# Attention outputs normalised by GpSimd instead of VectorE, with a new written-out order of the attention stage

## The chip, the cores and the metric

The kernel runs on one core of a Trainium2 chip. The metric is the device time of one execution in microseconds (us): the median of three runs, for the kernel before and for the changed kernel. The engines are named as in the profile: PE is TensorE (matmuls; PEld its weight loads), DVE is VectorE, ACT is ScalarE, POOL is GpSimd, SP is SyncE, whose queue issues the DMAs here.

## What is computed

A chain of four blocks over 1024 tokens of 512 features, each with a residual and a layer norm: a state-space scan, a gated feed-forward network, causal attention, and a feed-forward network with 4-bit weights. The change is inside the attention block:

```python
n_head = 32                      # head size 16, T = 1024, one sequence
q, k, v = proj(wq), proj(wk), proj(wv)
q, k = rope(q), rope(k)
scores = q @ k.T / 4             # causal: -inf above the diagonal
attn = softmax(scores)
out = (attn @ v) @ wo.T
```

## The kernel before

Before the attention stage the queries and keys lie in SBUF with the features of a head down the partitions (`q_st`, `k_st`): each pair of heads takes 128 partitions, one head in the upper 64 and one in the lower. The values lie by token (`v_tok`). The stage works on eight groups `g` of four heads, and on each group in two halves of 512 queries. Softmax takes the exact row maximum, so for a half the work has these steps; the letter is the one that stands for the step in the order string.

- `s`, search: PE multiplies a tile of 128 queries with up to 512 keys of a head (`search`, L741; on the diagonal two small matmuls add a mask, L745) into one of three PSUM banks (0 to 2, the "ring"), and DVE takes the row maximum from there (`maxima`, L1651). A group needs 12 searches for the first half and 28 for the second, 40 in all; those of group 0 are done earlier, beside the projections. 280 remain for the stage.
- `n`: DVE joins the maxima of the two key halves (`negate`, L1681). `t`: PE turns the maxima into a row in a ring bank (`turn_maxima`, L755), DVE copies it to SBUF (`keep_rows`, L1658), and two DMAs on SP's queue (`put_rows`, L427) put it into rows of `q_st`, so that the next matmul subtracts it.
- `k`, keys: PE multiplies a tile of 128 keys with the queries of the half for two or four heads (`keys`, L794) into banks 3 and 4, or 5 and 6, in turn; ACT takes the exponential (`exponentials`, L1178) into one of four buffers `p_t`. On the diagonal GpSimd zeroes a corner (`cut_corner`, L1322). For the last, narrowest tile of a half (`j` = 3 or 7) the four heads fill just 256 of the 512 columns of each of the two banks.
- `v`, values: PE multiplies the exponentials with the values and a column of ones (`values`, L810), summed over the half's key tiles in bank 7. The values come from `v_ring`, which GpSimd copies for a group (`ring_values`, L1315). Behind the last tile ACT copies bank 7 to `o_raw` (`keep_out`, L1164).
- `o`, out: PE transposes `o_raw` in four 128x128 pieces into a ring bank (`turn_out`, L819); DVE takes the reciprocal of the sums (`divide`, L1686) and multiplies (L1688) into `o_tok`.

Every engine walks the same list `ORDER` and does its own share of each step, so the list is the order of PE's queue and of the others'. It is made from three strings, HEAD, PATTERN (three times) and TAIL. Letters `x`, `y`, `z` near the end are DVE's dequantising of the first weight tiles of the last block (`nibbles`, `unscaled`, `weights_low`); GpSimd's multiplies with the scales (L1333, L1335) belong to them. Semaphores carry the waits: `ring_full` and `ring_read` for the ring, `st_full` and `exp_done` for the keys banks, `pv_step` for the values, `o_kept` for `o_raw`. The stage ends with PE transposing `o_tok` (L859), which waits until all outputs are read.

## Time and profile before

| | us |
|---|---|
| median of 3 runs | 849.19 (848.98 to 850.1) |
| the profiled execution, whole | 853.84 |
| its span, first to last instruction | 852.1 |
| attention stage in it (first keys to last output) | about 442 to 645 |

The profile is one execution. The page gives busy time by engine; views of the trace give the same for a stretch, for groups of like instructions, and instruction by instruction. A row names the source line, engine, operation, tiles written and read, shapes, and a count. In a timeline a row that merges several instructions gives the start of the first and the time until the end of the last. PSUM is `ps`, and most of SBUF is one tile, `arena`.

### The profile page before, as it was taken

Reading aid. Unit: us, or ns where it says so; the run is one execution under the profiler, and the core shown is the slowest. Engines: PE = TensorE matmul, PEld = TensorE weight load, DVE = VectorE, ACT = ScalarE, POOL = GpSimd, SP = SyncE. Lnnn points to the kernel's source line nnn. Section 1 sums busy time; section 2 is a strip of 40 time slices with the busy share of each in tenths; the row PEclk is TensorE's granted clock in tenths of the full one; section 3 lists DMA queues with packets and bytes.
Section 4 is the critical chain, followed back from the end, with each engine's and each line's share of the span. In section 5 each row is a group of like instructions: output and inputs, shape, how many; then the busy total and the mean of one; then the engine's idle time right before and its main releaser. Section 6 shows DMA issues by size and latency. Waiting matters only on the chain.

```text
span 852.1 us, 18986 instructions
## 1 busy us (share of the span) xinstructions
PE 788.1 (92%) x7930; PEld 372.6 (44%) x7930; DVE 628.5 (74%) x896; ACT 431.6 (51%) x579; POOL 297.7 (35%) x217
## 2 busy tenths in 40 slices
PE   8659787897999999999999999999998999999997
PEld 2434444444544444444334454444435544444444
DVE  3997999998556334456648999999976787774344
ACT  4876667564854331143236777787794633332100
POOL 0598898993103000058401222211242222221000
PEclk9597999999999999999999999999998999999999
DMA  7900000005331000039800000000232024320001
GB/s 216 379 2 3 3 3 3 3 3 173 99 90 28 1 0 1 1 55 192 149 1 2 2 2 1 2 2 2 63 120 61 1 92 125 124 81 0 13 37 50
DMA packets 53296, 46.62 MB, mean 55 GB/s; under 512 B 38289, under 2 KB 44241, under 8 KB 53218
## 3 DMA queue, kind: packets, MB, share of 16 engines
q1 hardware_dynamic: 53218, 45.49, 18.8%
q8 instruction: 60, 0.98, 0.5%
q14 instruction: 18, 0.15, 0.1%
HBM read 34.87 MB, written 2.16 MB: 43 GB/s over the span
## 4 chain that ended last, share of the span: by engine, by line
PE 71%; DVE 15%; ACT 5%; issue 5%; POOL 3%; SPq 1%; DMA 1%; DVEq 0%; ACTq 0%; POOLq 0%
PE ps L887 13%; PE ps L639 10%; PE ps L662 10%; PE ps L810 7%; DVE arena L1425 7%; PE ps L923 7%; PE ps L741 6%; PE ps L718 6%; PE ps L794 3%; DVE arena L1651 2%; PE ps L745 2%; PE ps L553 2%; PE ps L507 1%; POOL arena L1272 1%; ACT arena L1178 1%
## 5 line engine op out<-in xcount | busy, mean ns | idle before, releaser
L1651 DVE TENSOR_REDUCE arena<-ps 128x1 f16<-128x512 f32 (+3 forms) x320 | 182.4, 631 | 15.2 <-PE ps L741 7.3
L1178 ACT ACTIVATE arena<-ps 128x1024 f32<-128x1024 f32 (+2 forms) x160 | 142.5, 941 | 43.6 <-PE ps L794 42.8
L1272 POOL TENSOR_TENSOR arena<-arena 128x1024 f32<-128x1024 f32 x62 | 145.7, 2376 | 16.7 <-DVE arena L1425 11.5
L1425 DVE TENSOR_TENSOR_SCAN arena<-arena,ps 128x1024 f32<-128x1024 f32 x64 | 142.4, 2271 | 5.6 <-ACT arena L1019 3.0
L887 PE MATMUL ps<-arena 128*128 128x512 f16 x528 | 114.6, 379 | 0.1
L741 PE MATMUL ps<-arena 64*128 64x512 f16 (+3 forms) x384 | 97.1, 330 | 3.2 <-DVE arena L1658 1.2
L662 PE MATMUL ps<-arena 128*128 128x512 f16 (+1 forms) x464 | 97.6, 372 | 1.0 <-ACT arena L1096 1.0
L1322 POOL TENSOR_SCALAR_AFFINE_SELECT arena<-arena 128x512 f32<-128x512 f32 x64 | 42.7, 674 | 142.9 <-ACT arena L1178 142.8
L553 PE MATMUL ps<-arena 64*128 64x64 f16 x3072 | 60.0, 196 | 33.7 <-DVE arena L1425 30.4
L553 PEld LDWEIGHTS ps<-arena 64*128 64x128 f16 x3072 | 52.2, 98 | 85.0 <-DVE arena L1425 73.3
L639 PE MATMUL ps<-arena 128*128 128x512 f16 x384 | 88.8, 383 | 0.0
L1019 ACT ACTIVATE arena<-arena,negA 128x1024 f32<-128x1024 f32 x64 | 72.4, 1146 | 28.8 <-DVE arena L1425 26.9
L810 PE MATMUL ps<-arena 128*32 128x512 f32 (+3 forms) x768 | 82.1, 501 | 3.0 <-POOL arena L1322 3.0
L887 PEld LDWEIGHTS ps<-arena 128*128 128x128 f16 x528 | 51.6, 98 | 62.0 <-DVE arena L1766 0.6
L507 PE MATMUL ps<-arena,ident_sb 64*64 64x512 f32 x512 | 71.4, 633 | 2.1 <-POOL arena L1272 1.4
L794 PE MATMUL ps<-arena 64*128 64x512 f16 (+3 forms) x384 | 68.8, 326 | 0.9 <-ACT arena L1178 0.6
L662 PEld LDWEIGHTS ps<-arena 128*128 128x128 f16 x464 | 45.3, 98 | 51.7 <-ACT arena L1096 1.2
L741 PEld LDWEIGHTS ps<-arena 64*128 64x128 f16 x384 | 30.3, 93 | 71.5 <-DVE arena L1651 45.5
L923 PE MATMUL ps<-arena 128*128 128x512 f16 (+1 forms) x297 | 57.2, 355 | 0.0
L639 PEld LDWEIGHTS ps<-arena 128*128 128x128 f16 x384 | 36.2, 98 | 42.9 <-issue 3.3
L745 PE MATMUL ps<-mask_b,picks_b 64*128 64x64 bf16 (+1 forms) x512 | 53.0, 202 | 0.0
L1281 POOL COPY arena<-arena 128x512 f32 x24 | 14.8, 616 | 100.7 <-DVE arena L1520 46.0
(175 smaller groups left out, 960.7 us busy)
## 6 DMA issues: line engine op xcount, KB each, us to landing
arena<-in_w_q_dram SPq DMA_DIRECT2D x11, 768.0 KB, 4.1
arena<-c_rows SPq DMA_DIRECT2D x16, 512.0 KB, 10.9
arena<-in_w_s_dram SPq DMA_DIRECT2D x11, 384.0 KB, 4.9
arena<-in_x_fm_dram SPq DMA_DIRECT2D x8, 256.0 KB, 4.6
out_dram<-arena SPq DMA_DIRECT2D x8, 256.0 KB, 2.0
arena<-in_wg_dram SPq DMA_DIRECT2D x1, 1792.0 KB, 10.2
arena<-in_wu_dram SPq DMA_DIRECT2D x1, 1792.0 KB, 7.2
arena<-in_wd_dram SPq DMA_DIRECT2D x1, 1792.0 KB, 11.2
```

What stands on the lines that cost most here:

```text
L553: last = nc.tensor.matmul(ps[:, 2 * (i % 2) + r, q * SUB:(q + 1) * SUB], dtx_tok[c % 2][rows, s, q, :], diag[n][rows, e, q, :], start=(k = ...
L639: last = nc.tensor.matmul(banks(bank, 1), part[:, c, ds(t * P, P)], wsp[:, w, s, c, :], start=(c == 0 and part is src_h and s == 0), stop= ...
L662: last = nc.tensor.matmul(banks(bank, 1)[:, lo:hi], w[:, c, m * P:(m + 1) * P], part[:, c, h * HALF + lo:h * HALF + hi], start=(c == 0 and ...
L741: last = nc.tensor.matmul(dst, q_st[rows, 2 * g + r, i * P:(i + 1) * P], k_st[rows, 2 * g + r, key:key + w], start=True, stop=not diag)
L794: last = nc.tensor.matmul(ps[:, 3 + 2 * (e % 2) + b, at * (hi - lo):(at + 1) * (hi - lo)], k_st[rows, 2 * g + r, j * P:(j + 1) * P], q_st[ ...
L810: last = nc.tensor.matmul(ps[32 * a:32 * a + 32, 7, lo - HALF * half:HALF], v_ring[g % 2][:, j, a, :], p_t[n % 4][:, a, 0:hi - lo], start= ...
L887: last = nc.tensor.matmul(banks(bank + h, 1), gu[u][:, s, w * DC + c, :], part[:, c, h * HALF:(h + 1) * HALF], start=(c == 0 and s == 0 an ...
L923: last = nc.tensor.matmul(banks(u, 1)[:, lo:hi], part[:, m, ds(t * P, P)], wd1[:, s, m, lo:hi], start=(m == 0 and part is h1h and s == 0), ...
L1178: nc.scalar.activation(dst, src, ACT.Exp, scale=float(HD) ** -0.5).then_inc(exp_done, 1)
L1272: nc.gpsimd.tensor_tensor(hC[i % 4][:], hst[i % 3][:], c_all[:, n, :], ALU.mult).then_inc(hc_done, 1)
L1425: nc.vector.tensor_tensor_scan(hst[i % 3][:], dA[i % 3][:], banks(2 * (i % 2), 2), 0.0, ALU.mult, ALU.add).then_inc(scan_done, 1)
L1651: nc.vector.reduce_max(maxima_slot(half, k), ps[:, ring_bank(n), 0:len(heads) * w].rearrange("p (a w) -> p a w", a=len(heads)), AX, negate ...
```

## The change

- The outputs of a half no longer go through the ring, but for the last one of the stage. PE puts their four transposes into the free half of the two keys banks, as part of the keys step of the narrowest tile of a later half (`out_beside`: the outputs of (g, 0) beside keys (g, 1, 7), those of (g-1, 1) beside keys (g, 0, 3)). That step waits for `o_kept`.
- ACT copies the transposed outputs to SBUF (`o_copy`) right behind the exponential of that step; the keys step two further on, which writes the same banks, waits for this copy.
- DVE takes only the reciprocal, from SBUF (`invert`); GpSimd multiplies (`divide`), both at the new letter `d`.
- GpSimd walks `ORDER` as well. Its first ring copy is split in seven tiles and one, so that it no longer waits for all eight value tiles, and the copy for group 1 moves behind the first four corners.
- The searches of a half go in their natural order in place of the two written-out orders.
- `ORDER` is one string for the whole stage. ACT's `keep_out` no longer waits for the output of the group before.

```diff
-        r_den = view(199.75, 4 * GH, f32).rearrange("p (i a) -> p i a", i=4)
+        r_den = [view(199.75 + u / 16, 4 * GH, f32).rearrange("p (i a) -> p i a", i=4) for u in range(2)]
+        o_copy = [view(kb, HALF, f32) for kb in (120, 122)]
...
-        UNIT_ORDER = ((0, 1, 6, 8, 7, 3, 2, 9, 4, 11, 10, 5),
-                      (15, 4, 17, 13, 24, 5, 19, 26, 27, 12, 7, 10, 3, 8, 25, 20, 6, 9, 14, 0, 2, 21, 22, 11, 16, 1, 23, 18))
-        SEARCH = [[max_units(half)[k] for k in UNIT_ORDER[half]] for half in range(2)]
+        SEARCH = [max_units(half) for half in range(2)]
...
-        HEAD = ("kknntkkvkvsskssssssvssvsksskokssksskssksnsksvtskssvsskksvssksvskkssvssks"
...
+        ATTENTION = ("kkntssskskssvsksksssksksvkssvksvktssskssvsskkssvskkssvsskssvskssvsskkssskvnskdsssvskssktvsskskss"
...
+                     "svksskdsvsksvvskksssvksskvsksskvssksvtksskssskkssvskskdssvkvkntvkkvkkdxvvkvkkvkkvkvkkkyzvkkkvvvv"
+                     "do")
+
+        def out_beside(g, half, j):
+            if j != 4 * half + 3 or (g, half) == (0, 0):
+                return None
+            return (g, 0) if half else (g - 1, 1)
+        OUTS = 2 * NG - 1
...
                 if e >= 2:
                     pe.wait_ge(exp_done, e - 1)
+                    if out_beside(*EXP_STEP[e - 2]) is not None:
+                        g0, half0 = out_beside(*EXP_STEP[e - 2])
+                        pe.wait_ge(o_copied, 2 * g0 + half0 + 1)
...
+                if out_beside(g, half, j) is not None:
+                    g0, half0 = out_beside(g, half, j)
+                    pe.wait_ge(o_kept, 2 * g0 + half0 + 1)
+                    for b in range(4):
+                        i = 4 * half0 + b
+                        last = nc.tensor.transpose(ps[:, 3 + 2 * (e % 2) + b // 2, HALF // 2 + (b % 2) * P:HALF // 2 + (b % 2 + 1) * P],
+                                                   o_raw[:, i * P:(i + 1) * P], ident_sb[:])
                 last.then_inc(st_full, 1)
...
             pe.wait_ge(ring_read, EARLY + len(IN_RING))
+            pe.wait_ge(o_divided, OUTS)
...
-                if g:
-                    act.wait_ge(ring_read, RING_AT["out", g - 1, half] + 1)
...
+                if out_beside(g, half, j) is not None:
+                    g0, half0 = out_beside(g, half, j)
+                    if g0:
+                        act.wait_ge(o_divided, 2 * g0 + half0 - 1)
+                    nc.scalar.copy(o_copy[half0].rearrange("p (b q) -> p b q", b=2), ps[:, bank:bank + 2, HALF // 2:HALF]).then_inc(o_copied, 1)
...
-            pool.wait_ge(v_proj, TT)
-            pool.wait_ge(v_kept, TT)
...
+            def divide(g, half):
+                pool.wait_ge(r_made, 2 * g + half + 1)
+                src = o_copy[half].rearrange("p (i a d) -> p i a d", i=4, a=GH)
+                nc.gpsimd.tensor_tensor(o_tok[:, 4 * half:4 * half + 4, g * GH * HD:(g + 1) * GH * HD].rearrange("p i (a d) -> p i a d", a=GH),
+                                        src[:, :, :, 0:HD], r_den[half].unsqueeze(3).broadcast_to([P, 4, GH, HD]), ALU.mult).then_inc(o_divided, 1)
...
-            ring_values(0)
-            ring_values(1)
-            for g in range(NG):
-                for j in range(TT):
-                    cut_corner(g, j // 4, j)
-                    if j == 3 and 1 <= g < NG - 1:
-                        ring_values(g + 1)
...
+            ring_values(0, 0, TT - 1)
+            ring_values(0, TT - 1, TT)
+            for kind, g, half, *at in ORDER:
+                if kind == "divide":
+                    divide(g, half)
+                if kind != "keys" or not on_diagonal(half, at[0]) or at[1][-1] != 1:
+                    continue
+                cut_corner(g, half, at[0])
+                if at[0] == 3 and g < NG - 1:
+                    ring_values(g + 1)
...
+            def invert(g, half):
+                dve.wait_ge(o_copied, 2 * g + half + 1)
+                if g:
+                    dve.wait_ge(o_divided, 2 * g + half - 1)
+                src = o_copy[half].rearrange("p (i a d) -> p i a d", i=4, a=GH)
+                nc.vector.reciprocal(r_den[half].unsqueeze(3), src[:, :, :, HD:HD + 1]).then_inc(r_made, 1)
```

## Rows read from the trace of the kernel before

**Rows 1.** The page: the span, and busy us (share of the span) by engine.

```profile
span 852.1 us, 18986 instructions
PE 788.1 (92%) x7930; PEld 372.6 (44%) x7930; DVE 628.5 (74%) x896; ACT 431.6 (51%) x579; POOL 297.7 (35%) x217
```

**Rows 2.** Busy time by stretch: length, each engine's busy us (instructions), PE clock, DMA.

```profile
442.00:449.86 7.86, 5.93 (x57) 2.22 (x56) 0.41 (x2) 4.88 (x6) 2.51 (x5) 1.00 0.01 2
449.86:621.16 171.30, 169.69 (x1839) 75.78 (x1832) 169.09 (x321) 127.11 (x149) 37.44 (x60) 1.00 0.05 15
519.80:544.70 24.90, 24.76 (x275) 11.08 (x272) 24.57 (x48) 18.76 (x22) 5.63 (x10) 1.00 0.01 2
621.16:645.42 24.26, 20.07 (x185) 7.10 (x181) 15.83 (x24) 19.15 (x24) 13.48 (x10) 0.92 0.22 71
```

**Rows 3.** Groups by line and shape, 442 to 645.5 us: busy us, mean ns | idle before.

```profile
L1178 ACT ACTIVATE arena<-ps 128x1024 f32<-128x1024 f32 x112 | 110.0, 1027 | 32.9 <-PE ps L794 32.6 <-issue 0.2
L1651 DVE TENSOR_REDUCE arena<-ps 128x1 f16<-128x512 f32 x168 | 108.2, 684 | 1.2
L1322 POOL TENSOR_SCALAR_AFFINE_SELECT arena<-arena 128x512 f32<-128x512 f32 x64 | 42.7, 674 | 142.9 <-ACT arena L1178 142.8
L1164 ACT COPY arena<-ps 128x512 f32<-128x512 f32 x16 | 9.5, 593 | 7.1 <-PE ps L810 7.0
L1688 DVE TENSOR_TENSOR arena<-ps,arena 128x256 f32<-128x256 f32 x16 | 6.8, 424 | 0.6
```

**Rows 4.** Who waited for whom, 470 to 594.5 us: total us, times, longest.

```profile
PEld ps L741 <- DVE arena L1651: 30.3, 52, 0.8
PEld ps L741 <- DVE arena L1688: 6.7, 8, 0.8
```

**Rows 5.** DVE's instructions in order of time, 519 to 545 us: start, us.

```profile
522.89 0.17 DVE L1681 TENSOR_TENSOR arena<-arena 128x16 f16<-128x16 f16 x1
522.98 1.22 DVE L1651 TENSOR_REDUCE arena<-ps 128x2 f16<-128x256 f32 x3
...
526.74 0.25 DVE L1686 RECIPROCAL arena<-ps 128x16 f32<-128x16 f32 x1
527.02 0.42 DVE L1688 TENSOR_TENSOR arena<-ps,arena 128x256 f32<-128x256 f32 x1
527.48 5.63 DVE L1651 TENSOR_REDUCE arena<-ps 128x1 f16<-128x512 f32 x10
```

**Rows 6.** All engines in order of time at the stage's start, 441 to 462 us.

```profile
444.55 0.60 ACT L1150 ACTIVATE arena<-ps 128x512 f32<-128x512 f32 x1 [0.81 <-PE ps L639]
...
445.28 1.17 POOL L1315 COPY arena<-arena 128x512 f32<-128x512 f32 x2 [26.90 <-ACT arena L1150]
...
445.63 0.41 DVE L1658 COPY arena<-ps 4x512 f16<-4x512 f16 x1 [4.34 <-PE ps L755]
...
449.86 6.80 DVE L1651 TENSOR_REDUCE arena<-ps 128x2 f16<-128x256 f32 x13 [3.82 <-PE ps L745]
```

**Rows 7.** All engines in order of time in the tail, 616 to 646 us.

```profile
622.02 0.41 DVE L1658 COPY arena<-ps 4x512 f16<-4x512 f16 x1 [0.68 <-PE ps L755]
...
622.76 0.86 PE L810 MATMUL ps<-arena 128*32 128x256 f32 x16
...
625.68 0.61 PE L794 MATMUL ps<-arena 64*128 64x512 f16 x4
...
638.07 3.69 POOL L1322 TENSOR_SCALAR_AFFINE_SELECT arena<-arena 128x512 f32<-128x512 f32 x3 [0.84 <-ACT arena L1178]
...
638.60 2.07 DVE L1703 SCALAR_TENSOR_TENSOR arena<-arena 128x1536 f32<-128x1536 int32 x1
```

**Rows 8.** The chain that ended last, 440 to 530 us: values of 256 and 128 columns.

```profile
471.98 0.57 PE ps L810 x8
...
473.64 0.36 PE ps L810 x8
```

**Rows 9.** GpSimd's groups over the whole span, by shape.

```profile
L1302 POOL TENSOR_TENSOR arena<-arena 128x512 f16<-128x512 f32 x16 | 18.6, 1159 | 0.3
```

More of the change, by code:

```diff
@@ L185, in build @@
         st_full, exp_done, p_masked, pv_step, o_kept = sem("st_full"), sem("exp_done"), sem("p_masked"), sem("pv_step"), sem("o_kept")
+        o_copied, o_divided = sem("o_copied"), sem("o_divided")
         o_turned, oh_done, ol_done = sem("o_turned"), sem("oh_done"), sem("ol_done")
@@ L243, in exp_units @@
             return [(0, 1)] if 2 * (hi - lo) <= HALF else [(0,), (1,)]
+        EXP_STEP = [step for step in STEPS for _ in exp_units(*step[1:])]
         EXP_TO = list(itertools.accumulate(len(exp_units(half, j)) for _, half, j in STEPS))
@@ L265, in attention_order @@
                            if g or (half, k) not in EARLY_UNITS]),
-                "n": iter([("negate", g, half) for g, half in halves]),
+                "n": iter([("negate", g, 1) for g in groups]),
                 "t": iter([("turn", g, half) for g, half in halves if g or half]),
-                "o": iter([("out", g, half) for g, half in halves]),
+                "d": iter([("divide", n // 2, n % 2) for n in range(OUTS)]),
+                "o": iter([("out", NG - 1, 1)]),
                 "x": iter([("weights", 0, 0)]), "y": iter([("weights", 1, 0)]), "z": iter([("weights", 2, 0)])}
             order = []
-            for letter in HEAD + 3 * PATTERN + TAIL:
+            for letter in ATTENTION:
                 step = next(streams[letter])
@@ L1306, in _, with ring_values @@
                     stack(2 * k + u, u)
-            pool.wait_ge(v_proj, TT)
-            pool.wait_ge(v_kept, TT)
             pool.wait_ge(v_ones, 2)
-            def ring_values(g):
+            def ring_values(g, lo=0, hi=TT):
                 if g >= 2:
                     pool.wait_ge(pv_step, STEP_AT[g - 1, 0, 0])
-                nc.gpsimd.tensor_copy(v_ring[g % 2][:, :, :, 0:HD],
-                                      v_tok[:, :, g * GH * HD:(g + 1) * GH * HD].rearrange("p i (a d) -> p i a d", a=GH)).then_inc(v_ringed, 1)
+                pool.wait_ge(v_kept, hi)
+                last = nc.gpsimd.tensor_copy(v_ring[g % 2][:, lo:hi, :, 0:HD],
+                                             v_tok[:, lo:hi, g * GH * HD:(g + 1) * GH * HD].rearrange("p i (a d) -> p i a d", a=GH))
+                if hi == TT:
+                    last.then_inc(v_ringed, 1)
+            def divide(g, half):
[3 more added lines that the diff above has]
+                                        src[:, :, :, 0:HD], r_den[half].unsqueeze(3).broadcast_to([P, 4, GH, HD]), ALU.mult).then_inc(o_divided, 1)
             def cut_corner(g, half, j):
@@ L1678, in negate @@
             def negate(g, half):
-                if half:
-                    dve.wait_ge(ring_read, searched(g, 1))
-                    nc.vector.tensor_tensor(m_neg[1][:], m_neg[1][:], m_b[:], ALU.min).then_inc(m_joined, 1)
+                dve.wait_ge(ring_read, searched(g, half))
+                nc.vector.tensor_tensor(m_neg[half][:], m_neg[half][:], m_b[:], ALU.min).then_inc(m_joined, 1)
+            def invert(g, half):
[4 more added lines that the diff above has]
+                nc.vector.reciprocal(r_den[half].unsqueeze(3), src[:, :, :, HD:HD + 1]).then_inc(r_made, 1)
             def divide(g, half, n):
@@ L1685, in divide @@
                 src = ps[:, ring_bank(n), :].rearrange("p (i a d) -> p i a d", i=4, a=GH)
-                nc.vector.reciprocal(r_den[:].unsqueeze(3), src[:, :, :, HD:HD + 1]).then_inc(r_made, 1)
+                nc.vector.reciprocal(r_den[half].unsqueeze(3), src[:, :, :, HD:HD + 1]).then_inc(r_made, 1)
                 dve.wait_ge(r_made, 2 * g + half + 1)
                 nc.vector.tensor_tensor(o_tok[:, 4 * half:4 * half + 4, g * GH * HD:(g + 1) * GH * HD].rearrange("p i (a d) -> p i a d", a=GH),
-                                        src[:, :, :, 0:HD], r_den[:].unsqueeze(3).broadcast_to([P, 4, GH, HD]),
+                                        src[:, :, :, 0:HD], r_den[half].unsqueeze(3).broadcast_to([P, 4, GH, HD]),
                                         ALU.mult).then_inc(ring_read, 1)
@@ L1725, in _ @@
                     keep_rows(g, half, RING_AT[kind, g, half])
+                elif kind == "divide":
+                    invert(g, half)
                 elif kind == "out":
+                    dve.wait_ge(o_divided, OUTS - 1)
                     divide(g, half, RING_AT[kind, g, half])
```

17 lines of the change are left out of this document (7 added, 10 removed).

## The prediction

> **What bounds the kernel now.** I read the page's summary first: PE is busy 92% of 852.1 us, DVE 74% [rows 1]. Such shares are averages over stages, so I next cut the attention stage, the only one that the diff touches, into stretches [rows 2]. The reader is to see there one engine that is full in the long middle stretch: from 449.86 to 621.16 us DVE is busy 169.09 of 171.30 us, and in a settled period of 24.90 us (one group of four heads) 24.57 us. PE shows nearly the same (24.76), but its ends are modelled, so that number can't decide between the two. The waits do [rows 4]: in five periods PE's weight loads for the maxima search (L741) sat 30.3 us behind DVE's reductions (L1651), and 6.7 us more behind the normalising multiply (L1688). PE waits for DVE to empty a ring bank; DVE hardly waits for PE. So this stretch is set by DVE: 280 reductions (40 of them for each of seven groups), the turn copies and the normalising of outputs.
>
> The two ends of the stage have other bounds. At the start DVE stands still until 449.86 us, after its one small copy at 445.63 [rows 6]: PE, in order, has values to do that wait for GpSimd's ring copies, and those began only when ScalarE had kept the eighth value tile. At the end, from 621.16 to 645.42 us, no search is left; ScalarE is busy 19.15 of 24.26 us [rows 2], and the last 7 us are a chain through GpSimd's corners, the last values, copy, transposes and division.
>
> **The change, part by part.**
>
> *Outputs leave the ring.* Today an output costs DVE a reciprocal (starts 526.74), a multiply (527.02) and the next reduction starts at 527.48: 0.74 us [rows 5]. Eleven of the sixteen outputs lie in front of the last search in the old order (counted in its letters), so they take 11 x 0.74 = 8.1 us of the bound stretch. After the change DVE keeps a reciprocal of 16 numbers a partition, from SBUF, and 13 of those stand in front of the last search. The trace has no such reciprocal. Its bounds: below, the `negate` step, also 16 numbers from SBUF, takes 0.09 us from its start to the next one's [rows 5]; above, today's reciprocal with the wait for its own result, 0.28 us. I take 0.15, nearer the lower end because the wait on its own result goes away: 13 x 0.15 = 2.0 us (1.2 to 3.6). Net -6.1 us (-6.9 to -4.5).
>
> *ScalarE's copies.* A copy of 128x512 from PSUM lasts 593 ns (L1164) [rows 3]; 15 are added. In the bound stretch ScalarE is busy 127.11 of 171.30 us, so 13 x 0.59 = 7.7 us lie in its idle time: cost 0. If that cover were gone each would delay the keys two steps on, which now wait for the copy as well as for the exponential.
>
> *GpSimd's multiplies.* 256 numbers a partition. Upper bound: the 512-wide two-input op at 1.16 us (L1302) [rows 9]; lower: half of a ring copy (two of 512 take 1.17 us [rows 6]), 0.3 us. GpSimd is busy 5.6 of 24.9 us in a period [rows 2], so two of them (0.6 to 2.3 us) fit. Behind the divide's wait for DVE's reciprocal only corner cuts are queued. I looked where the divides stand in the new order: after each, the next corner's values are three or four values away, some 4 us; cost 0. What could change that is contention: at 638.60 a DVE op of 2.07 us and at 638.07 three corners lasting 3.69 us lie beside each other, where one corner takes 0.67 on the mean [rows 3, 7]. So GpSimd and DVE do hold each other up in this kernel when both read SBUF; if a new reciprocal always met a busy GpSimd (6.9 of 24.9 us with the divides, 28%) it would lose up to 0.64 us, 13 x 0.28 x 0.64 = 2.3 us. I put that in the range, not in the sum.
>
> [...]
>
> *PE's transposes* (four for an output) are moved from a ring step into a keys step: the same work, 0 us. They bring a new wait: the keys step with the transposes stands in PE's queue until ScalarE has copied bank 7 (`o_kept`); queued behind it are the next searches, which feed DVE. From the last values to that keys step the new order has, in the tight cases of the bound stretch, two to four searches and a key between, 1.2 us and more of DVE's pace, against an exponential in progress (1.03 us) and the copy (0.59) [rows 3]. What is left, 0.4 us, is under what three full ring banks give DVE (3 x 0.6 us). Cost 0 in the sum; it is the rival below.
>
> *The order.* (a) The start: the searches now stand before the first values, behind two keys and a turn. PE can reach them when the turn copy is done at 446.04 instead of 449.86 [rows 6]: -3.8 us (at least -2.8, if PE, at its start, is a microsecond late). GpSimd's split of the first ring copy removes the wait for tile 8 in front of the first corner, and the second group's copy (0.6 us) moves behind four corners; this lies beside DVE's searches now, so 0. (b) The middle: priced by rows, no stretch of PE work between two searches is over 1.8 us in the new order (in the old one four are, all at the start or in the tail), so the ring's cover holds. The 96 values form 83 unbroken runs instead of 92; two values in one run take 0.86 us for 256 and 128 columns where they take 0.57 + 0.36 apart [rows 7, 8], so PE wins 9 x 0.07 = 0.6 us, which DVE hides: 0. (c) The turns: each is a copy on DVE and two DMAs on SP's queue, then keys that wait for them. In the tail this takes at most 3.7 us from the copy (622.02) to the first keys (625.68) [rows 7]; the new order leaves six or seven searches (3.6 to 4.2 us) and some keys between, the old one seven. 0, with a bound of 7 x 0.3 us. (d) Natural search order alternates the two row halves strictly; the same reductions, 0. (e) Behind the last search stand 18 keys and 15 values in both orders. (f) The dropped wait in `keep_out` was never late in the rows: 0.
>
> *The tail* gains a ScalarE copy inside its run of exponentials (+0.6 us); the second new copy comes after the last exponential, beside corners and values. DVE's dequantising starts behind a reciprocal that waits for that copy, about 1 us later, and may push the corners by as much. In its favour three outputs leave DVE. +0.6 (-0.5 to +1.5).
>
> **Sum.** -3.8 - 6.1 + 0.6 = -9.3 us. On the profiled execution 852.1 becomes 842.8 us; that execution took 853.84 in all and the runs' median is 849.19, so the difference is put on the median: 849.19 - 9.3 = 839.9 us.
>
> **The rivals.**
> - *More than that.* DVE's 2.2 us of idle time in the stretch [rows 2] and the late reductions behind each output (PE's 6.7 us on L1688 came 8 times [rows 4], about 0.15 us of it reaches DVE, 11 x 0.15 = 1.7) go too, because three banks serve the search all the time. -9.3 - 3.9 = -13.2: 836.0 us. For it: the new order is even. Against: a new order makes its own gaps.
> - *PE becomes the bound.* Its 24.76 us of 24.90 are taken at their word; the stretch then shrinks by 0.14 us a period, 1 us in seven, and only the start and that are won: -3.8 - 1.0 + 0.6 = -4.2, 845.0 us. For it: the modelled share, and the trace can't tell PE's slack. Against: 37 us of weight loads waiting for DVE in five periods.
> - *Slower: the outputs' new loop.* In each output PE waits for ScalarE's keep, ScalarE for PE's transposes, and the keys two steps on for ScalarE's copy. If the ring doesn't cover it, an output loses up to 1.03 + 0.59 = 1.6 us of PE's time, 13 x 1.6 = 20.8; it decides against the change from 9.3 / 13 = 0.7 us an output. At 1.0 us: +13 - 9.3, 852.9 us. For it: PE takes its steps in order and the distances are down to two searches. Against: ScalarE's 44 us of idle time and the ring's depth.
> - *Nothing measurable.* Half of that loop's loss, 0.7 us an output, eats the whole gain: 849.
>
> **How the numbers follow.** Forecast (838 to 843) 0.45, more 0.20, PE bound 0.20, nothing 0.06, slower 0.09. The range reaches to both neighbours: low end -3.8 - 6.9 - 3.9 - 0.1 = -14.7, 834.5; high end, with -2.8 at the start, -4.5 for the outputs, +2.3 of contention, +1.5 in the tail and no more, -3.5, 845.7, and a little for PE: 846.5. Faster by over 0.2% (about what a measurement here tells from no change) 0.85, within 0.06, slower 0.09.
>
> **What would show it.** Right: the first reduction at about 446 us, no 128x256 multiply on DVE but one, the last search ending near 611 us, DVE still over 97% busy until there, a period near 23.7 us, and a tail of 24 to 26 us. Wrong: DVE idle over 6 us in the searches, with PE's releaser ScalarE's copy or the transposes' line; keys waiting for DMA; or a tail over 27 us with GpSimd last.

## The result and the profile after

The changed kernel takes 844.19 us (median of six runs, 842.83 to 847.18), the kernel before 849.33 us in the runs beside it. The ratio is 0.9947 (95% interval 0.993 to 0.9964): 5.1 us faster, 0.5%, where 9.3 us were forecast (839.9 us). The profiled execution took 847.18 us, and its span fell by 6.6 us:

```profile
span 845.5 us, 18993 instructions
PE 783.0 (93%) x7930; PEld 368.7 (44%) x7930; DVE 621.9 (74%) x881; ACT 439.2 (52%) x594; POOL 305.9 (36%) x233
```

Over the whole span DVE lost 6.6 us of work against [rows 1], nearly the fall of the span. That is a coincidence, as the cut into stages shows. These times are differences between marks that both traces have (us):

| from one mark to the next | before | after | difference | forecast |
|---|---|---|---|---|
| start of the run to the down projection of the first feed-forward block (FFN) | 312.77 | 311.95 | -0.8 | 0 |
| to the stage's first keys (projections, early searches) | 128.44 | 126.75 | -1.7 | 0 |
| to the stage's first reduction | 8.64 | 4.80 | -3.8 | -3.8 |
| search stretch: first to last reduction of the stage | 171.27 | 173.52 | **+2.2** | **-6.1** |
| tail, to the first final transpose | 24.29 | 22.67 | -1.6 | +0.6 |
| output projection, to the last FFN's first matmul | 28.21 | 27.31 | -0.9 | 0 |
| to the end | 178.50 | 178.49 | 0 | 0 |

So the stretch that was to gain most became longer, and three pieces that were costed at nothing or as a small loss gave 4.2 us. The first row isn't a gain of the change: all kernels of this document do the same work up to there, and their profiled executions take 307.6 to 312.8 us for it. The view by stretch of the kernel after (columns: length, then busy us with instructions for PE, PEld, DVE, ACT and POOL, granted PE clock, DMA share, GB/s) shows the start, the search stretch, one settled period and the tail; its counterpart is [rows 2]:

```profile
438.69:443.49 4.80, 4.11 (x33) 1.84 (x32) 0.47 (x3) 3.02 (x4) 1.32 (x3) 1.00 0.00 2
443.49:617.00 173.51, 171.69 (x1881) 76.97 (x1878) 165.32 (x313) 137.55 (x167) 46.06 (x76) 1.00 0.03 8
541.72:566.60 24.88, 24.80 (x273) 11.31 (x272) 23.81 (x46) 19.81 (x26) 6.79 (x12) 1.00 0.01 2
617.00:639.67 22.67, 17.43 (x170) 5.51 (x163) 13.17 (x19) 19.13 (x24) 13.52 (x13) 1.00 0.37 125
```

Read the second line against 171.30 and 169.09 us of [rows 2]: DVE has 3.8 us less to do in the stretch, and stands still for 8.2 us where it stood still for 2.2. The period is as long as before (24.88 against 24.90 us) with DVE busy 23.81 instead of 24.57. DVE no longer sets the stretch by itself. The forecast's signs of being right fail here: the last search ends at 617.0 us and not near 611, and DVE is busy for 95% of the stretch and not for over 97%. Who waits, in the same stretch (columns: who waits, for whom, us in total, times, longest):

```profile
PEld ps L749 <- DVE arena L1684: 43.5, 90, 0.8
ACT arena L1195 <- PE ps L805: 33.0, 50, 1.7
PEld ps L805 <- ACT arena L1195: 8.2, 14, 0.8
DVE arena L1691 <- PE ps L763: 4.7, 3, 4.3
DVE arena L1684 <- PE ps L753: 3.3, 12, 0.6
DVE arena L1684 <- PE ps L749: 2.8, 11, 0.4
PEld ps L828 <- ACT arena L1195: 2.6, 8, 0.4
```

The same view of the kernel before, from 449.86 to 621.16 us, has these rows for the same waits:

```profile
PEld ps L741 <- DVE arena L1651: 45.5, 83, 0.8
DVE arena L1651 <- PE ps L745: 3.8, 1, 3.8
PEld ps L794 <- ACT arena L1178: 0.4, 2, 0.2
PEld ps L810 <- ACT arena L1178: 0.4, 2, 0.2
```

New are DVE's waits for PE's searches (L753, L749; 6.1 us; before, the 3.8 us are the wait ahead of the stage's first reduction, and after, 4.3 of the 4.7 us on L763 also lie ahead of it) and PE's waits for ScalarE's exponentials (10.8 us where they were 0.8). Still there, 43.5 us, is the row of [rows 4] on which "PE waits for DVE" was built. It can't mean that here, with DVE idle for 8 us; the experiments show what it means.

The added operations, by group over the attention stage (columns: line, engine, operation, shapes, count; busy us, mean ns; idle before):

```profile
L1345 POOL TENSOR_TENSOR arena<-arena 128x256 f32<-128x256 f32 x15 | 9.3, 619 | 9.7 <-DVE arena L1721 9.7
L1200 ACT COPY arena<-ps 128x512 f32<-128x512 f32 x15 | 8.8, 586 | 0.0
L1721 DVE RECIPROCAL arena<-arena 128x16 f32<-128x16 f32 x15 | 3.7, 244 | 2.6 <-ACT arena L1200 2.6
```

All three sizes are as forecast: 619 ns for a division on GpSimd (0.3 to 1.16 us were given), 586 ns for a copy (593), and a reciprocal that lasts 244 ns but lets the next instruction start 0.16 us after its own start (0.15 taken), as in DVE's timeline of the kernel after (start, us):

```profile
525.50 0.24 DVE L1721 RECIPROCAL arena<-arena 128x16 f32<-128x16 f32 x1
525.66 5.79 DVE L1684 TENSOR_REDUCE arena<-ps 128x1 f16<-128x512 f32 x10
```

Of the 13 reciprocals in the search stretch none ran beside a busy GpSimd (one overlaps it by 16 ns). The two in the tail did, beside corners: the first lasted 255 ns, the second, from 635.82 us, 253 ns (timeline of the tail, cut):

```profile
619.91 1.22 POOL L1352 TENSOR_SCALAR_AFFINE_SELECT arena<-arena 128x512 f32<-128x512 f32 x2 [0.77 <-ACT arena L1195]
620.85 0.26 DVE L1721 RECIPROCAL arena<-arena 128x16 f32<-128x16 f32 x1 [2.55 <-ACT arena L1200]
...
633.29 3.58 POOL L1352 TENSOR_SCALAR_AFFINE_SELECT arena<-arena 128x512 f32<-128x512 f32 x3 [0.95 <-ACT arena L1195]
```

### The profile page after: what moved, and what is told of

It reads as the page before. It is cut to its first block, busy times and chain, and to the rows that moved or that the text cites. A ratio compares the mean times of both kernels' runs of the same rounds, so it can differ in the third digit from the quotient of the medians.

```text
span 845.5 us, 18993 instructions
## 1 busy us (share of the span) xinstructions
PE 783.0 (93%) x7930; PEld 368.7 (44%) x7930; DVE 621.9 (74%) x881; ACT 439.2 (52%) x594; POOL 305.9 (36%) x233
## 4 chain that ended last, share of the span: by engine, by line
PE 69%; DVE 16%; issue 5%; ACT 5%; POOL 2%; DMA 1%; SPq 1%; DVEq 0%; ACTq 0%; POOLq 0%
PE ps L906 13%; PE ps L670 10%; PE ps L647 9%; PE ps L828 8%; DVE arena L1458 7%; PE ps L942 7%; PE ps L726 6%; PE ps L749 6%; PE ps L805 4%; DVE arena L1684 2%; PE ps L561 2%; PE ps L753 2%; PE ps L515 1%; POOL arena L1294 1%; ACT arena L1195 1%
## 5 line engine op out<-in xcount | busy, mean ns | idle before, releaser
L1195 ACT ACTIVATE arena<-ps 128x1024 f32<-128x1024 f32 (+2 forms) x160 | 143.6, 942 | 36.7 <-PE ps L805 33.8
L749 PE MATMUL ps<-arena 64*128 64x512 f16 (+3 forms) x384 | 91.6, 329 | 3.3 <-DVE arena L1684 1.3
L828 PE MATMUL ps<-arena 128*32 128x512 f32 (+3 forms) x768 | 79.6, 496 | 0.8 <-POOL arena L1352 0.6
L805 PE MATMUL ps<-arena 64*128 64x512 f16 (+3 forms) x384 | 68.2, 327 | 2.8 <-ACT arena L1195 2.4
L749 PEld LDWEIGHTS ps<-arena 64*128 64x128 f16 x384 | 30.4, 93 | 60.8 <-DVE arena L1684 43.5
L753 PE MATMUL ps<-mask_b,picks_b 64*128 64x64 bf16 (+1 forms) x512 | 49.8, 202 | 0.0
```

What stands on the lines that cost most here:

```text
L749: last = nc.tensor.matmul(dst, q_st[rows, 2 * g + r, i * P:(i + 1) * P], k_st[rows, 2 * g + r, key:key + w], start=True, stop=not diag)
L805: last = nc.tensor.matmul(ps[:, 3 + 2 * (e % 2) + b, at * (hi - lo):(at + 1) * (hi - lo)], k_st[rows, 2 * g + r, j * P:(j + 1) * P], q_st[ ...
L828: last = nc.tensor.matmul(ps[32 * a:32 * a + 32, 7, lo - HALF * half:HALF], v_ring[g % 2][:, j, a, :], p_t[n % 4][:, a, 0:hi - lo], start= ...
L1195: nc.scalar.activation(dst, src, ACT.Exp, scale=float(HD) ** -0.5).then_inc(exp_done, 1)
```

## The experiments

e1 to e6 and e8 were executed once each, e7 and e9 to e15 five to ten times; every stretch below is that of one profiled execution.

**How much room has PE, and how much DVE?** Two edits, each on both kernels. `light`: the reductions read only half the columns, so the row maxima are those of half the keys. `nomask`: the searches leave out the causal mask's matmuls.

```diff
-  ...ps[:, ring_bank(n), 0:len(heads) * w].rearrange("p (a w) -> p a w", a=len(heads)),
+  ...ps[:, ring_bank(n), 0:len(heads) * w].rearrange("p (a w) -> p a w", a=len(heads))[:, :, 0:w // 2],
...
-                                            start=True, stop=not diag)
-                    if diag:
+                                            start=True, stop=True)
+                    if False:
```

> The kernel before, with DVE's maxima taken over half of each search's columns (so the subtracted number isn't the row's true maximum): some 68 us less DVE work in the stretch from the first to the last search of the attention stage, which was 171.3 us. If DVE sets that stretch, as the prediction said, it falls until ScalarE (127 us busy in it) is in the way: 130 to 140 us. If PE's own work sets it nearly as much, it stays over 160 us.

> The changed kernel with the same halved maxima (the subtracted number isn't the row's true maximum). The stretch of searches was 173.5 us. If DVE still sets it: 130 to 145 us. If PE sets it: 163 to 173 us, hardly below the same cut of the kernel before, since PE's work is the same in both. If keys waiting for ScalarE's exponentials and copies set it: unchanged, 170 to 174 us, and later than the kernel before with the same cut.

> The kernel before without the two small mask matmuls on diagonal searches (the maximum then covers future keys as well): some 19 us less PE work in the stretch of searches (448 matmuls, 128 and 64 columns), DVE's work the same. If DVE sets the stretch: 171 us, less than 1.5 us shorter. If PE sets it nearly as much: 166 to 168 us, where DVE's own work of 165 us stops it.

> The changed kernel without the mask matmuls (the maximum covers future keys as well): 19 us less PE work. If PE sets the stretch of 173.5 us: 159 to 164 us, close to DVE's own 157. If DVE or ScalarE's copies set it: over 171 us.

> The changed kernel with both cuts at once: maxima over half of the columns and no mask matmuls (the subtracted number is neither the true maximum nor masked). With the halved maxima alone the stretch of searches was 165.0 us. If what was left there is PE's own work, the 19 us of mask matmuls come off it: 146 to 154 us. If it is ScalarE (136 us busy) or keys waiting for its exponentials and copies: 161 to 165 us.

Measured, search stretch and whole time (before: 171.3 and 850.1 us; after: 173.5 and 844.2):

| | search stretch | whole |
|---|---|---|
| e1, before, light | 163.2 | 841.6 |
| e2, after, light | 165.0 | 834.5 |
| e3, before, no mask | 170.1 | 847.4 |
| e4, after, no mask | 169.3 | 839.7 |
| e5, after, both | 159.0 | 826.4 |

The views by stretch of e1, e2 and e5:

```profile
445.42:608.59 163.17, 162.24 (x1838) 71.29 (x1832) 113.59 (x321) 125.49 (x149) 36.70 (x59) 1.00 0.05 15
438.32:603.33 165.01, 163.61 (x1871) 72.86 (x1868) 103.94 (x313) 135.68 (x166) 45.61 (x75) 1.00 0.03 7
436.26:595.21 158.95, 154.07 (x1428) 51.69 (x1428) 103.60 (x313) 134.69 (x166) 45.69 (x75) 1.00 0.02 7
```

And PE's longest row of waits in e1, from the view of who waits for whom:

```profile
PEld ps L741 <- DVE arena L1651: 48.5, 76, 0.8
```

In e1 DVE's work fell by 55 us and the stretch by only 8.1. What is left, 163 us before and 165 us after, is what PE and the engines other than DVE need; the two orders hardly differ in that. So in the kernel before PE stood 8 us behind DVE, no more, and the most that any relief of DVE could win in that order was those 8 us. PE's busy time fell with it, from 169.69 to 162.24 us, for the same matmuls (x1839 and x1838): a "busy" PE isn't a PE at its limit. Taking PE's mask work away gave 1.2 us before and 4.2 us after: before, PE was not the limit; after, it counts. In the kernel after the two limits lie at 165.0 us (e2) and 165.3 us (DVE's busy time), and the stretch takes 173.5. The 8 us between belong to neither engine alone. e4 (169.3) and e5 (159.0) fell between the cases that their expectations gave: against e2, e5's PE is busy 9.5 us less and its stretch is 6.1 us shorter, with PE idle for 4.9 us and DVE for 55. So what is left in e2 isn't PE's work alone, and which engine or buffer holds the rest isn't shown.

e1 also settles the row of waits. DVE is busy 70% of the stretch there, and yet PE's weight loads "wait for DVE" for 48.5 us, more than the 45.5 before. Its timeline shows how:

```profile
500.26 1.90 DVE L1651 TENSOR_REDUCE arena<-ps 128x2 f16<-128x128 f32 x5 [0.19 <-PE ps L745]
...
501.62 0.16 PEld L810 LDWEIGHTS ps<-arena 128*32 128x32 f32 x8 [0.42 <-issue]
501.62 1.06 PE L810 MATMUL ps<-arena 128*32 128x512 f32 x8
502.62 0.09 PEld L741 LDWEIGHTS ps<-arena 64*128 64x128 f16 x1 [0.84 <-DVE arena L1651]
```

The load at 502.62 is put down to a reduction, but the reductions had ended at 502.16, and PE was streaming values (L810) until 502.68. A wait of 0.84 us is what a 512-wide values step leaves between its last weight load (501.78) and its modelled end, and 0.8 us is the longest of these waits in before, after and e1 alike. Laying all idle times over 60 ns of the search's weight loads over PE's matmuls in the kernel before gives 59.3 us of idle loads in the stretch, 57.9 of them beneath running matmuls, 48.6 beneath values. PE's new rows in the kernel after are no different: all but 0.1 of the 10.8 us put down to ScalarE lie beneath running matmuls. What such a row can't give is the room: 1.3 us of the idle loads before lie beneath no matmul, and e1 found 8. The search's load starts 0.06 us ahead of the values' modelled end; the values' own eight loads are done by 501.78, beneath the first four of their eight matmuls. What holds the search's load until then isn't shown.

**What are the parts worth in either order?** The outputs' path changed in two places: the transposes moved from a ring step to a keys step, and the multiplication moved from DVE to GpSimd. The order changed beside it. Four kernels fill the table between before and after (e6, e9, e15, e14). e6 is the changed kernel with the multiplication back on DVE, reading ScalarE's copy:

```diff
-                if kind == "divide":
-                    divide(g, half)
...
+                dve.wait_ge(r_made, 2 * g + half + 1)
+                nc.vector.tensor_tensor(o_tok[...], src[:, :, :, 0:HD], r_den[half]..., ALU.mult).then_inc(o_divided, 1)
```

> The changed kernel with the normalising multiply back on DVE, but from the SBUF copy and not from a ring bank; GpSimd doesn't multiply. DVE gets 13 x 0.5 to 0.6 us back in the stretch of 173.5 us. If DVE alone sets it: 180 us. If PE alone sets it: 173 to 174. If the two take turns, since each has nearly the same work and only three banks lie between them: 175 to 178.

e9 is the new path in the old order and the old search order, with a `d` where an `o` stood or right behind the keys that carry the transposes; e15 is e9 with the multiplication back on DVE, by e6's edit.

```diff
-        SEARCH = [max_units(half) for half in range(2)]
+        UNIT_ORDER = ((0, 1, 6, 8, 7, 3, 2, 9, 4, 11, 10, 5),
+                      (15, 4, 17, 13, 24, 5, 19, ...))
+        SEARCH = [[max_units(half)[k] for k in UNIT_ORDER[half]] for half in range(2)]
...
-        ATTENTION = ("kkntssskskssvsksksssksksvkssvksvktssskssvsskkssvskkssvsskssvskssvsskkssskvnskdsssvskssktvsskskss"
+        ATTENTION = ("kkntkkvkvsskssssssvssvsksskksskssksskssksvtskssvsskksvssksvskkssvssksvdsksksvnskssvtsksskssvsskk"
```

> The engine move alone: outputs leave by the key banks, ScalarE and GpSimd as in the changed kernel, but the letters and the search order are those of before (a reciprocal stands where an output stood, or right behind the keys step that carries its transposes). The start is that of before, 8.2 to 8.6 us from the first keys to the first search. Theory A, the terms stand by themselves and the move is worth its 6.1 us in any order: the search stretch falls from 171.3 to 165.2 us and the total to about 843. Theory B, DVE and PE have nearly equal loads, and what DVE gains by the move counts only in an order laid out for it: replaying the steps with the traces' durations, the stretch comes out at about 173 us, the total between 848 and 851. If B holds, the start and the new order must bring what the changed kernel has won.

> The new path in the old order (stretch 174.1 us), with the multiplication put back on DVE from ScalarE's copy, none on GpSimd: 13 multiplications of about 0.46 us, 6 us of DVE's work, are back in the stretch. Against the kernel before (171.3 us) only the place of the transposes and ScalarE's copy differ. Theory A, a multiplication less on DVE is worth its 6 us in any order, and it is the place of the transposes that costs in the old one: stretch about 180 us. Theory B, in the old order DVE's relief counts in part only, since PE is what is late there: stretch 175 to 178 us. If it comes out at 171 to 174, the transposes' place costs nothing and GpSimd's part of the path does.

e14 is the kernel before with the new order alone: the new letters with an `o` for each `d`, and the natural search order.

> The kernel before with the new letters and the natural search order, and nothing else: the outputs stay a step of the ring, transposed there and multiplied on DVE, at the places of the new string's d. This is the new order by itself. First search 4.8 us after the first keys. Theory 'order': the new order suits only the new path; stretch 179 to 182 us, as with the multiplication put back on DVE (179.6), total 849 to 853. Rival: the 8.3 us of that run came from the transposes beside the keys, not from the order; stretch 171 to 174 us, total 842 to 846.

Search stretch, in brackets the whole:

| | all as before | transposes beside the keys, ScalarE's copy | and the multiplication on GpSimd |
|---|---|---|---|
| old order | 171.3 (849.3, before) | 178.0 (854.8, e15) | 174.1 (849.5, e9) |
| new order | **182.7** (855.5, e14) | 179.6 (849.7, e6) | **173.5** (844.2, after) |

The views by stretch of e15, e14 and e6:

```profile
444.59:622.63 178.04, 171.44 (x1847) 76.35 (x1840) 169.34 (x321) 132.79 (x162) 37.55 (x60) 1.00 0.05 14
440.00:622.72 182.72, 177.33 (x1881) 77.78 (x1878) 172.43 (x326) 131.79 (x154) 39.46 (x64) 1.00 0.03 8
439.96:619.55 179.59, 174.59 (x1883) 77.15 (x1880) 171.07 (x326) 138.84 (x167) 39.49 (x64) 1.00 0.03 8
```

The relief of DVE is worth 3.9 us in the old order and 6.1 in the new. The place of the transposes costs 6.8 us in the old order and gives 3.1 in the new. The order by itself costs 11.4 us in the stretch; e14 starts its searches 3.8 us earlier, and over the stage, from the first keys to the first final transpose, it loses 6.7 (210.9 us; before 204.2, e9 205.1, after 201.0). So the new path without the new order is worth nothing (e9's ratio 0.9999, 0.9985 to 1.0013), the new order without the new path is a loss (e14's 1.0061, 1.0039 to 1.0083), and only together are they a gain. DVE's idle time in the stretch says the same: 2.2 us before, 8.7 in e15, 9.6 in e9, 10.3 in e14, 8.5 in e6 and 8.2 after. Either part of the change breaks what the old pair had. e14 and e15 missed what was expected of them: e14 is a little over its theory 'order' (179 to 182), e15 at the upper end of theory B. e6 came out where DVE alone would set the stretch (180), though in the same order a DVE with much less to do (e2) wins only 8.5 us. Two reservations: the new letters weren't made for a ring step at `d`, nor the old ones for transposes beside the keys; and 13 outputs fall in the stretch of all these kernels, where before has 11.

What DVE's relief met in the old order, from e9's view by stretch and from its waits in that stretch:

```profile
445.44:619.53 174.09, 170.32 (x1847) 76.45 (x1840) 164.54 (x310) 132.54 (x162) 44.11 (x71) 1.00 0.05 14
```

```profile
ACT arena L1197 <- PE ps L814: 7.0, 7, 1.8
DVE arena L1686 <- PE ps L755: 6.4, 8, 3.5
```

DVE has 4.6 us less to do than before and idles 9.6 us (3.5 of the 6.4 us on L755 lie ahead of the stretch). ScalarE waits 7.0 us in seven places for keys steps that are handed over only behind their transposes (L814); in the kernel after that is 1.1 us in one place. The timeline of one output in e9 (all engines, start and us):

```profile
537.26 1.06 PE L830 MATMUL ps<-arena 128*32 128x512 f32 x8
...
538.26 0.71 PE L807 MATMUL ps<-arena 64*128 64x256 f16 x8
538.68 0.69 DVE L1686 TENSOR_REDUCE arena<-ps 128x1 f16<-128x512 f32 x1 [0.41 <-PE ps L751]
...
538.90 0.66 PE L814 MATMUL ps<-ident_sb,arena 128*128 128x128 f32 x4
...
539.49 0.39 PE L751 MATMUL ps<-arena 64*128 64x512 f16 x2
...
539.92 0.69 DVE L1686 TENSOR_REDUCE arena<-ps 128x1 f16<-128x512 f32 x1 [0.54 <-PE ps L751]
```

From 537.26 to 539.49 PE does a values step, a keys step and four transposes with one search among them; DVE empties the ring and waits twice, 0.41 and 0.54 us. As a ring step the same 0.66 us of transposes gave DVE 0.74 us of work; beside the keys PE still pays for them and DVE gets nothing.

**Are the letters and the search order a pair?** e7 gives the kernel before the natural search order, e8 gives the changed kernel the old one (the two `SEARCH` lines of e9's diff, alone).

> The kernel before with the searches in natural order and nothing else. The prediction gave this 0 us. If the strict alternation of the two row halves lets PE overlap neighbours, the part between the down projection of the first feed-forward block and the first keys, where 40 searches lie between projections, gets 1 to 2 us shorter (it was 128.4 us, 126.7 in the changed kernel); in the attention stage, where a search waits for DVE's bank anyway, under 1 us. By the prediction: no difference over 0.3 us in either.

> The changed kernel with the old written-out order of searches inside a half and nothing else. If the natural order is worth PE time: the part in front of the first keys 1 to 2 us longer than 126.7 us, and the stretch of searches (173.5 us), where PE counts, 2 to 5 us longer. By the prediction: no difference over 0.3 us.

e7: stretch 178.8 us (+7.5), 852.9 us, ratio 1.0042 (1.0026 to 1.0059), 0.4% slower. e8: stretch 179.2 us (+5.6), 852.7 us. They are a pair. A reading of why, which no run isolates: a 512-wide search off the diagonal is one matmul on PE (384 ns) for 684 ns on DVE, while a diagonal one of two heads with 128 columns is six overlapping matmuls on PE (two each of 220, 216 and 189 ns) for 416 ns on DVE. Which of them stands beside a values step would then decide whether the ring is full when PE turns away. In e7 DVE waits for masked searches (L743) in 24 places, the first of them (3.8 us) ahead of the stretch; before, that first one is the only one in the view.

```profile
DVE arena L1649 <- PE ps L743: 10.7, 24, 3.8
```

e7 also shows the 1.7 us of the projections: from the down projection to the first keys it takes 126.75 us like the kernel after, e8 takes 128.37. The early searches run better in the natural order: every kernel here that has it, and does all the work, takes 126.73 to 126.81 us there, every one with the old order 128.35 to 128.53.

**Is the start worth its 3.8 us?** e10 is the kernel before with searches ahead of the first values:

```diff
-        HEAD = ("kknntkkvkvsskssssssvssvsksskok...
+        HEAD = ("kknntssskskssvksvskssvsvksskok...
```

> The kernel before with its first 25 letters rearranged: searches stand ahead of the first values. First search 4.8 us after the first keys instead of 8.6 under every theory. Theory A, as the prediction had it, DVE's 3.8 us are won in full: stretch still 171.3 us, total 3.8 us below before, 845.5. Theory B, the five keys and two values that PE did in that time only move into a stretch where PE has little room: the stretch grows by 1 to 2 us, the total is 2 to 2.5 us below, 847. Theory C, PE is the bound: the stretch grows by all of 3.2 to 3.8 us, total unchanged.

848.16 us, ratio 0.9977 (0.9957 to 0.9997). The first reduction comes 4.79 us after the keys, and the stretch grows by 1.9 us, to 173.1. Half of the 3.8 us is given back: DVE starts early, but PE's keys and values of those microseconds now stand in the stretch.

**Is the mechanism or the order to blame for the 8 us?** e11 is the changed kernel with another letter string and another order of the searches of groups 1 to 7, the early ones left natural, laid out so that neither engine should stand still:

```diff
+        UNIT_ORDER = ((7, 0, 11, 10, 9, 6, 1, 4, 3, 2, 5, 8),
+                      (12, 19, 23, 24, 17, 11, 13, 18, 5, 10, 9, 22, 1, 16, 4, 27, 7, 8, 15, 26, 2, 3, 6, 14, 21, 0, 25, 20))
-        ATTENTION = ("kkntssskskssvsksksssksksvkssvksvktssskssvsskkssvskkssvsskssvskssvsskkssskvnskdsssvskssktvsskskss"
+        ATTENTION = ("kkntsskksssvsskskssskkssvsksksvsskskvtsksssksvssvssksksvskssskksvsskksdsvsnsvsskssvvtsksksskssks"
```

> The changed kernel with another letter string and another order of the later groups' searches, laid out so that neither PE nor DVE stands still (early searches keep their natural order). Nothing of the work, the banks or the engines differs. Theory 'order': the 8.3 us that the new order cost are a matter of which search stands beside which value, and come back in part: by the traces' durations the stretch should be 167 to 169 us instead of 173.5, and the total 4 to 6.5 us below the changed kernel, 838 to 840. Rival 'mechanism': the new path of the outputs (PE waiting for ScalarE's keep and copy, GpSimd beside DVE) costs this in any order: stretch 172 to 174 us, total 843 to 845.

```profile
439.90:610.24 170.34, 168.59 (x1882) 78.52 (x1877) 165.27 (x312) 137.04 (x167) 46.08 (x76) 1.00 0.05 15
```

The stretch falls by 3.2 us to 170.3, DVE's idle time to 5.1, and the whole to 842.65 us, ratio to before 0.9915 (0.9884 to 0.9945). It lies between what the two theories gave: order brings back 3.2 of the 8.2 us; the whole misses the 838 to 840 us that theory 'order' gave. Of the kernels that do all the work this is the fastest, though its interval overlaps that of the changed kernel.

**Is it ScalarE's new copy?** PE's 10.8 us of waits for ScalarE suggest it, though nearly all of them lie beneath running matmuls. e12 copies only the 17 columns of each head that are used, e13 makes each copy twice, first into a spare place:

```diff
-  nc.scalar.copy(o_copy[half0].rearrange("p (b q) -> p b q", b=2), ps[:, bank:bank + 2, HALF // 2:HALF]).then_inc(o_copied, 1)
+  nc.scalar.copy(o_copy[half0].rearrange("p (b x d) -> p b x d", b=2, d=32)[:, :, :, 0:HD + 1],
+                 ps[:, bank:bank + 2, HALF // 2:HALF].rearrange("p b (x d) -> p b x d", d=32)[:, :, :, 0:HD + 1]).then_inc(o_copied, 1)
```

```diff
+  nc.scalar.copy(o_spare[half0].rearrange("p (b q) -> p b q", b=2), ps[:, bank:bank + 2, HALF // 2:HALF])
   nc.scalar.copy(o_copy[half0].rearrange("p (b q) -> p b q", b=2), ps[:, bank:bank + 2, HALF // 2:HALF]).then_inc(o_copied, 1)
```

> The changed kernel, ScalarE's copy of an output takes only the 17 columns of each head that are used, not all 32: 272 numbers a partition instead of 512. From the exponentials' rows (1027, 811 and 597 ns for 1024, 768 and 512) ScalarE takes about 0.84 ns more a number, so a copy should fall from 586 to about 385 ns, 2.6 us over the 13 in the search stretch. Theory 'ScalarE's loop' (PE's weight loads wait on ScalarE for 10.8 us in the stretch where they waited for 0.8 before, because of the copies): the stretch falls by 1.5 to 2.6 us, from 173.5 to 171 to 172, total about 842. Rival 'matching' (what is lost is DVE and PE running dry by turns, ScalarE has slack): stretch within 0.5 us of 173.5, total within 1 us of 844.

> The changed kernel, with each of the 15 copies of ScalarE done a second time into a spare place, ahead of the one that counts: 0.59 us more in the loop from the transposes to the keys two steps on, 7.6 us over the 13 in the search stretch. Theory 'ScalarE's loop': the stretch grows by most of it, 5 to 7.6 us, total 849 to 852. Rival 'matching': ScalarE was busy 137.6 of 173.5 us, the second copy lies in its idle time, and the stretch grows by under 2 us, total 844 to 846.

The copy in e12, by group:

```profile
L1200 ACT COPY arena<-ps 128x272 f32<-128x272 f32 x15 | 6.0, 401 | 0.0
```

401 instead of 586 ns, and the stretch 173.41 instead of 173.52 us (843.51 us in all). With 7.6 us of copies more, e13's stretch is 174.58, +1.1 us (844.36 us). ScalarE has the room that the prediction gave it; its copy is not what holds the stretch up.

## Why the prediction was wrong

The step that failed is the order, costed at nothing ("the middle": (b) and (d)), and with it the premise under the whole sum, that DVE alone sets the stretch and PE has time to spare. In its place the runs show a PE 8 us behind DVE and an order that by itself costs 11.4 us in the stretch (e14). The stretch grew by 2.2 us where it was to fall by 6.1. That the total lies as near as 4.3 us to the forecast is luck: between the two profiled executions 5.6 of those 8.3 us came back in pieces that were costed at nothing or as a loss (the early searches, the tail, spells of the clock).

- **The start, -3.8: right at the mark, worth half.** The first reduction came 3.84 us earlier after the keys, by the step described; e10 shows 1.9 of it given back in the stretch. The sum took DVE's idle time for a gain, on the reading that PE had time to spare.
- **The outputs, -6.1: a size without its condition.** Taking the multiplication off DVE gives 6.1 us in the new order (e6 against after), 3.9 in the old; the whole path gives 9.2 in the new (e14 against after) and costs 2.8 in the old (e9). "PE's transposes: the same work, 0" is wrong in both: with ScalarE's copy, +6.8 in one order, -3.1 in the other. The term was computed as a property of DVE's queue and is one of DVE and PE together.
- **"The middle: 0" is the step that failed**, (b) and (d) of the order. The new order was costed at nothing because no stretch of PE's work between two searches is over 1.8 us and because the same reductions are done. By itself it costs 11.4 us (e14), its natural search order alone 7.5 (e7). Looking for the longest gap between searches wasn't enough: that cover holds only where the ring is full at the start of a gap, and nothing in the working showed that it is. Why the order costs so much isn't shown beyond that.
- **What misled it was one reading**: 37 us of "weight loads waiting for DVE" in five periods [rows 4], taken for PE's slack, and used again against the rival "PE becomes the bound". Nearly all of it (36.7 us) lies beneath PE's own matmuls. PE's slack was 8 us in the whole stretch (e1), 1.2 us a group.
- **That rival** (845.0 us) came nearest in time. That is luck as well. It was right that little room is left on PE, but not as little as 24.76 of 24.90 us in [rows 2] say (0.14 us a group; e1 found 1.2), and it was wrong that the stretch would shrink by a microsecond, since it grew by 2.2. "More than that" fell: DVE's idle time grew instead of going.
- **The rival of a slower output loop** had the right place, PE's transposes between two searches, and named a link that isn't the costly one: ScalarE's copy is covered (e12, e13). In the order of the change the loop's exponentials wait 1.1 us for the transposes; in the old order, 7.0.
- **Costs put at nothing that held**: ScalarE's copies (e12, e13), and GpSimd's divisions, for which nothing on PE or DVE is seen to wait. The 2.3 us of contention kept for the range were not needed: the reciprocals of the stretch met no busy GpSimd, and the two of the tail that did took 255 and 253 ns where the others took 241 to 247. The pair that the prediction read at 638 us does lengthen: in the kernel before, the DVE op (L1703) took 2.07 us beside busy corners and 1.76 in each of its ten executions without them, and the last corner beside it took 2.15 us where the median is 0.64. That this holds whenever both read SBUF isn't shown, and the two reciprocals beside corners, hardly longer than the others, speak against it.
- **The tail, +0.6 forecast, -1.6 measured.** About 0.9 of it goes with the clock: the same tail takes 23.3 to 23.4 us in e7 and e10, at 0.99 and 1.00 of full clock where before has 0.92. The remaining 0.7 us come with the new path (22.65 in e9 too, but 22.90 in e11), where a loss was forecast.
- **Not seen at all**: 1.7 us by the natural order of the early searches, and 0.9 us behind the stage, which is the clock. The change doesn't touch the code behind the stage, so those 0.9 us can't be counted on.

Taken together, the start (3.84 less the 2.25 of the stretch, in which path and order about cancel: 1.6), the early searches (1.7) and the tail without the clock (0.7) make 4.0 of the 5.1 us of the medians; the clock can have given the rest (2.6 us of the 6.6 between the two profiled executions are the tail's 0.9, the 0.9 behind the stage and the 0.8 ahead of it). What stays open is the 8.2 us of DVE's idle time after: e11 recovers 3.2 by order alone. Whether a fourth ring bank would bring the stretch near 165 us wasn't tried: the eight banks of the kernel's `ps` tile are taken (three for the ring, four for the keys, one for the values).

## What to carry to other kernels

Before relief of a full engine is counted as a gain, measure the room of the next one by making the full engine's work artificially light: here that gave 8 us, and the forecast had spent 9.9 (3.8 and 6.1). Where two engines feed each other through a few buffers and their loads come within a few per cent, as here, a step's worth depended on the order around it, and the order tuned for one balance lost when the balance moved; cost path and order together. An idle weight load that named another engine wasn't room on PE here (nearly all of 59.3 us lay beneath running matmuls), and the part beneath no matmul wasn't the room either (1.3 us, where e1 found 8).

## What the runs showed of the hardware

The granted clock moved without the change asking for it. In the kernel before PE was granted half of full clock from about 641.4 to 648.3 us (0.50 in the view of 641.50 to 648.20 us; with it the shares 0.63 and 0.78 below are 4.0 of 5.42 and 2.9 of 6.58 us at that level). It had been busy 7.36 of the 8 us up to 640, and was busy 2.60 of the next 5.42. The kernel after ran through the same piece at 1.00 of full clock. The views by stretch, before and then after (columns as above; the number ahead of the DMA share is the share of full clock):

```profile
632.00:640.00 8.00, 7.36 (x62) 1.78 (x54) 6.65 (x8) 6.97 (x9) 3.88 (x4) 1.00 0.50 161
640.00:645.42 5.42, 2.60 (x25) 1.32 (x21) 2.04 (x5) 1.87 (x2) 4.82 (x3) 0.63 0.01 3
645.42:652.00 6.58, 6.57 (x38) 5.47 (x39) 4.49 (x8) 4.88 (x9) 0.00 (x0) 0.78 0.64 194
```

```profile
632.00:640.00 8.00, 5.22 (x57) 2.26 (x54) 4.69 (x6) 4.94 (x7) 7.02 (x6) 1.00 0.19 55
640.00:645.42 5.42, 5.26 (x38) 3.77 (x37) 4.37 (x8) 4.95 (x9) 0.52 (x1) 1.00 0.65 201
645.42:652.00 6.58, 6.58 (x32) 2.96 (x31) 3.96 (x9) 1.93 (x5) 0.00 (x0) 1.00 0.10 29
```

The stretch behind the stage takes 27.3 us at 1.00 of full clock (after, e6, e9) and 28.2 to 29.4 us where a spell at the lower level falls into it (before, e7, e10, e11, e13; 0.90 to 0.95). Which kernel has it isn't explained by the busy time of its tail: e11's tail (PE busy 17.2 of 22.9 us) is followed by a spell, the tail after (17.4 of 22.7) is not. So 0.9 us here are neither won nor lost by the change for a reason that these runs show.
